# x updated earlier in one cross attention, a new order in grouped attention, and the last MX batch in pieces

## The reference

```python
x = x + _L0_attn_ref(_layernorm(x), Wqkv, Wout)                    # causal, 16 heads
x = x + _L0_xattn_ref(_layernorm(x), ctx, Wq, Wk, Wv, Wo, gq, gk)  # q and k normed by head
x = x + _L0_ffn_ref(_layernorm(x), router, shared, routed)
x = x + _L1_attn_ref(_layernorm(x), Wq, bq, Wk, bk, Wv, bv, Wo, bo) # 32 query heads in 8 groups
x = x + _L1_xattn_ref(_layernorm(x), ctx, mask, Wq, Wk, Wv, Wo)     # masked keys
x = x + _L1_ffn_ref(_layernorm(x), gate_w, up_w, down_w)            # MX
...
scales = jnp.maximum(max_abs / _FP8_MAX, _EPS)      # _mx_dequant, blocks of 32
q = (blocks / scales[..., None]).astype(jnp.float8_e4m3fn).astype(jnp.float32)
return (q * scales[..., None]).reshape(rows, feat)
```

## Time and profile before

| | |
|---|---|
| median of three runs | 1590.43 us |
| the profiled execution | 1583.99 us |
| its span on the core | 1582.2 us |
| PE busy | 1479.4 us, 93% |
| DVE busy | 1068.8 us, 68% |
| ACT busy | 968.4 us, 61% |
| POOL busy | 730.6 us, 46% |
| mean granted TensorE clock | 0.986 |

### The profile page before, as it was taken

One profiled execution on the slowest core, in us unless ns is written; L12 is line 12 of the kernel. 1 busy time (PEld: TensorE's weight loads), 2 busy tenths in 40 slices (PEclk: granted clock), 3 DMA queues, 4 the chain that ended last, 5 costly groups with the idle time before them and its releaser, 6 DMA issues. The chain is left out here.

```text
span 1582.2 us, 30300 instructions
## 1 busy us (share of the span) xinstructions
PE 1479.4 (93%) x10256; PEld 1214.4 (77%) x10256; DVE 1068.8 (68%) x2468; ACT 968.4 (61%) x2611; POOL 730.6 (46%) x893
## 2 busy tenths in 40 slices
PE   5999889999999999899987989899999999989998
PEld 2666568888888888688874555489999999977886
DVE  4667667878877787554446777655556665588886
ACT  2766657777777777433236777577777777642221
POOL 3666635555555555223333333213444434457775
PEclk9999999999999999999999999999999999999999
DMA  6000020000000000000011000020000000000000
GB/s 243 2 1 2 2 95 5 3 5 3 5 3 5 3 3 1 22 1 1 1 53 82 2 1 1 15 90 8 8 8 8 5 4 5 1 1 14 14 14 14
DMA packets 15609, 29.82 MB, mean 19 GB/s; under 512 B 1505, under 2 KB 12002, under 8 KB 14690
## 3 DMA queue, kind: packets, MB, share of 16 engines
q1 hardware_dynamic: 15458, 27.89, 4.8%
HBM read 25.79 MB, written 2.10 MB: 18 GB/s over the span
## 5 line engine op out<-in xcount | busy, mean ns | idle before, releaser
L1444 POOL TENSOR_TENSOR weights_even<-weights_even,cross_reciprocal 128x512 f32<-128x512 f32 x64 | 66.7, 1042 | 202.8 <-DVE cross_reciprocal L1676 202.8
L926 POOL TENSOR_TENSOR cross_work<-cross_work,cross_reciprocal 128x512 f32<-128x512 f32 x64 | 66.6, 1040 | 182.6 <-DVE cross_reciprocal L1083 182.6
L1526 ACT ACTIVATE weights_even<-bank,cross_shift 128x128 f32<-128x128 f32 x256 | 90.7, 366 | 80.0 <-DVE cross_shift L1668 80.0
L1149 PE MATMUL bank<-ident,cross_work 128*128 128x128 f32 x768 | 117.0, 275 | 2.4 <-DVE cross_work L1061 2.4
L979 ACT ACTIVATE cross_work<-bank,cross_shift,cross_q_rms 128x128 f32<-128x128 f32 x256 | 113.6, 456 | 2.2 <-DVE cross_shift L1055 2.2
L1149 PEld LDWEIGHTS bank<-ident,cross_work 128*128 128x128 f32 x768 | 90.5, 142 | 26.9 <-DVE cross_work L1061 18.0
L2468 DVE TENSOR_REDUCE grouped_maxima<-bank 128x4 bf16<-128x512 f32 x128 | 82.4, 685 | 34.5 <-PE bank L2550 26.9
L1953 POOL TENSOR_TENSOR mlp_low_inner<-mlp_inner,mlp_high_inner 128x512 fp32r<-128x512 f32 x36 | 48.7, 1354 | 117.1 <-ACT mlp_high_inner L1996 117.1
L1666 DVE TENSOR_REDUCE cross_maxima<-bank 128x4 f32<-128x512 f32 x64 | 44.2, 690 | 84.5 <-PE bank L1809 84.5
L402 POOL TENSOR_TENSOR causal_masked_maxima<-causal_maxima,causal_constants 128x512 bf16<-128x512 bf16 x64 | 67.0, 1068 | 55.7 <-DVE causal_maxima L547 55.7
L2808 ACT ACTIVATE mx_silu<-bank 128x512 f32<-128x512 f32 x32 | 19.1, 598 | 114.7 <-PE bank L2928 114.6
(11 more groups left out here) (365 smaller groups left out, 5332.9 us busy)
## 6 DMA issues: line engine op xcount, KB each, us to landing
weights_even<-in_weights SPq DMA_DIRECT2D x2, 2560.0 KB, 11.7
weights_even<-in_weights SPq DMA_DIRECT2D x2, 1732.0 KB, 8.6
weights_odd_early<-in_weights SPq DMA_DIRECT2D x1, 3072.0 KB, 11.7
weights_odd_values<-in_weights SPq DMA_DIRECT2D x1, 3072.0 KB, 18.5
weights_odd_late<-in_weights SPq DMA_DIRECT2D x2, 1536.0 KB, 10.0
x<-in_x SPq DMA_DIRECT2D x4, 512.0 KB, 8.1
...
```

The source lines that it names most:

```text
L926: pool.tensor_tensor(probs[x], probs[x], reciprocal[x][:, :].unsqueeze(2).to_broadcast([P, PER, P]), ALU.mult).then_inc(probs_divided, 1)
L1149: last = pe.transpose(bank[:, j * P:(j + 1) * P], source, core.ident[:, :])
L1444: pool.tensor_tensor(probs[x], probs[x], reciprocal[x][:, :].unsqueeze(2).to_broadcast([P, JOBS, P]), ALU.mult).then_inc(probs_divided, 1)
L1526: last = act.activation(probs[x][:, j, :], bank_scores[x][:, j * P:(j + 1) * P], ACT.Exp, scale=SCALE, bias=shift[x][:, j:j + 1], accum_ou ...
```

## The change

- In the first cross attention, DVE's update_x(t - 1) at g == 2 moves from after sum_q to ahead of row_maxima, right after make_low_heads.
- The scale step gets its two numbers from a new pair of columns in SBUF, scale_bounds, that POOL fills once in the setup. It is used in all places that scale.
- In grouped attention PE's order within a step becomes: key and query projections, scores (1, 1), weigh_values of the batch before (1), scores_transposed (0), turn_maxima (1), the values' projection, turn_out, project_heads, scores (0, 0) of the next batch, scores_transposed (1), scores (0, 1) of the next, turn_h, turn_heads, weigh_values (0), turn_maxima (0) of the next, scores (1, 0) of the next. The turned maxima of half 0 go to the bank bank_scoresT[0], which adds a wait for the exponential that last read it. DVE and ACT get a matching order: maxima (1, 1), statistics one batch later than before, spread (1), normalise_heads, update_x, the next batch's maxima (0, 0) and (0, 1), spread (0), maxima (1, 0); ACT's copy_outT goes ahead of the first four exponentials. POOL's rstd is one batch later.
- In the last batch of the MX MLP the second half is rounded by DVE in two pieces of 256 columns, instead of by POOL in one of 512; PE turns and ACT copies each piece by itself, and the down projection's matmuls go between. add_to_x of the batch before goes ahead of the rounding.

```diff
@@ -246,6 +247,8 @@
             pool.memset(core.ones_bf[:, :], 1.0)
+            pool.memset(core.scale_bounds[:, 0:1], 1.0 / FP8_MAX)
+            pool.memset(core.scale_bounds[:, 1:2], LEAST_SCALE)
             pool.memset(core.ones[:, :], 1.0).then_inc(made, 1)
@@ -755,11 +758,17 @@
-def dve_scale(dve, source, scratch, step, least, done):
+def dve_block_scale(dve, core, scratch):
+
+    return dve.tensor_scalar(scratch.scale[:, :], scratch.largest[:, :], core.scale_bounds[:, 0:1],
+                             core.scale_bounds[:, 1:2], ALU.mult, ALU.max)
+
+
+def dve_scale(dve, core, source, scratch, step, done):
...
                            ALU.max, apply_absolute_value=True))
-    step(dve.tensor_scalar(scratch.scale[:, :], scratch.largest[:, :], 1.0 / FP8_MAX, least, ALU.mult, ALU.max))
+    step(dve_block_scale(dve, core, scratch))
     step(dve.reciprocal(scratch.inverse[:, :], scratch.scale[:, :]))
@@ -1113,6 +1122,8 @@
                         make_low_heads(i - 2, g % 2)
+                    if g == 2 and batch_there(t - 1):
+                        update_x(t - 1)
                     if there(i):
@@ -1127,8 +1138,6 @@
                         sum_q(i + 1, (g + 1) % 2)
-                    if g == 2 and batch_there(t - 1):
-                        update_x(t - 1)
                     if there(i + 2):
@@ -2266,6 +2273,7 @@
         bank_scores, bank_scoresT, bank_out, bank_misc = core.banks[0:2], core.banks[2:6], core.banks[6], core.banks[7]
+        turned_maxima = [bank_scoresT[0][:, 0:P], bank_scores[0][:, 0:P]]
@@ -2424,11 +2432,11 @@
                     normalise(t + 2)
+                if batch_there(t - 1):
+                    copy_outT(t - 1)
                 if batch_there(t):
...
                         exponentials(t, 0, j)
-                if batch_there(t - 1):
-                    copy_outT(t - 1)
                 if batch_there(t + 1):
@@ -2475,7 +2483,7 @@
                     dve.tensor_tensor(shifts[c][:, :, :],
-                                      bank_scores[0][:, 0:P].unsqueeze(1).to_broadcast([P, PER, P]),
+                                      turned_maxima[c].unsqueeze(1).to_broadcast([P, PER, P]),
                                       row_of_member.unsqueeze(2).to_broadcast([P, PER, P]), ALU.mult)\
@@ -2510,20 +2518,20 @@
                 if batch_there(t):
-                    row_maxima(t, s, 1, 0)
                     row_maxima(t, s, 1, 1)
+                if batch_there(t - 3) and not left_to_next(t - 3):
+                    statistics(t - 3)
+                if batch_there(t):
                     spread_shifts(t, 1)
...
                     normalise_heads(t - 1)
-                if batch_there(t + 1):
-                    row_maxima(t + 1, 1 - s, 0, 0)
                 if batch_there(t - 2):
...
                 if batch_there(t + 1):
+                    row_maxima(t + 1, 1 - s, 0, 0)
                     row_maxima(t + 1, 1 - s, 0, 1)
                     spread_shifts(t + 1, 0)
-                if batch_there(t - 2) and not left_to_next(t - 2):
-                    statistics(t - 2)
+                    row_maxima(t + 1, 1 - s, 1, 0)
                 if isinstance(t, int) and t == -1:
@@ -2542,8 +2550,8 @@
                 pe.wait_ge(max_ready, nonneg(GROUPS * b + SLOTS * c + 2 * pair))
-                if pair == 0:
-                    pe.wait_ge(shifts_ready, nonneg(EC * b + c))
+                if c == 0 and pair == 0:
+                    pe.wait_ge(shifts_ready, nonneg(EC * b))
                 for j in range(2):
@@ -2562,7 +2570,9 @@
                 pe.wait_ge(max_ready, GROUPS * b + SLOTS * (c + 1))
-                pe.matmul(bank_scores[0][:, 0:P], maxima[s][:, c, :, :].rearrange("p j m -> p (j m)"),
+                if c == 0:
+                    pe.wait_ge(probs_ready, nonneg(GROUPS * b - SLOTS + 1))
+                pe.matmul(turned_maxima[c], maxima[s][:, c, :, :].rearrange("p j m -> p (j m)"),
                           core.minus_ident_bf[:, :], start=True, stop=True).then_inc(max_turned, 1)
@@ -2646,21 +2656,20 @@
                 if batch_there(t):
-                    scores(t, s, 1, 0)
-                    scores_transposed(t, s, 0)
                     scores(t, s, 1, 1)
...
                     weigh_values(t - 1, 1 - s, 1)
+                if batch_there(t):
+                    scores_transposed(t, s, 0)
+                    turn_maxima(t, s, 1)
                 if batch_there(t + 1):
...
                     project_values(t + 1)
-                if batch_there(t):
-                    turn_maxima(t, s, 1)
+                if batch_there(t - 1):
+                    turn_out(t - 1)
                 if batch_there(t - 2):
                     project_heads(t - 2)
-                if batch_there(t - 1):
-                    turn_out(t - 1)
                 if batch_there(t + 1):
@@ -2680,6 +2689,7 @@
                     turn_maxima(t + 1, 1 - s, 0)
+                    scores(t + 1, 1 - s, 1, 0)
             batches(pe, step)
@@ -2691,6 +2701,9 @@
     SCALE_STEPS = 5
+    VERY_LAST, PIECES = BATCHES - 1, 2
+    PIECE = INTER // HALVES // PIECES
+    TILES_A_PIECE = PIECE // P
     with ExitStack() as ctx:
@@ -2764,7 +2780,7 @@
                 pool.wait_ge(innerT_filled, nonneg(HALVES * (b - 1)))
-                for j in range(HALVES):
+                for j in range(HALVES if b != VERY_LAST else HALVES - 1):
                     pool.wait_ge(inner_scaled, HALVES * b + j + 1)
@@ -2819,6 +2835,13 @@
+            def copy_last_piece(k):
+                act.wait_ge(last_turned, k + 1)
+                first = TILES // HALVES + TILES_A_PIECE * k
+                act.activation(innerT[:, first:first + TILES_A_PIECE, :],
+                               last_banks[k][:, 0:PIECE].rearrange("p (i t) -> p i t", t=P),
+                               ACT.Copy).then_inc(last_copied, 1)
+
             fetch_h(0)
@@ -2827,8 +2850,11 @@
                         silu_of_gate(HALVES * (t - 1) + j, j)
-                    if batch_there(t - 2):
+                    if batch_there(t - 2) and (t - 2, j) != (VERY_LAST, 1):
                         copy_innerT(t - 2, j)
+                if t - 2 == VERY_LAST:
+                    for k in range(PIECES):
+                        copy_last_piece(k)
                 if isinstance(t, int) and t == 1:
@@ -2858,7 +2884,24 @@
                 dve.wait_ge(inner_rounded, nonneg(i - HALVES + 1))
-                dve_scale(dve, bank_gate[j][:, :], scratch[j], inner_step, LEAST_SCALE, inner_scaled)
+                dve_scale(dve, core, bank_gate[j][:, :], scratch[j], inner_step, inner_scaled)
+
+            def round_last_half():
+                dve.wait_ge(inner_scaled, HALVES * BATCHES)
+                dve.wait_ge(innerT_filled, HALVES * (VERY_LAST - 1))
+                for k in range(PIECES):
+                    part = slice(k * PIECE, (k + 1) * PIECE)
+                    blocks = slice(k * PIECE // BLOCK, (k + 1) * PIECE // BLOCK)
+                    scaled, rounder = scratch[1].scaled[:, part], scratch[1].rounder[:, part]
+                    dve.tensor_tensor(scaled, scaled, rounder, ALU.add).then_inc(last_chain, 1)
+                    dve.wait_ge(last_chain, 2 * k + 1)
+                    dve.tensor_tensor(scaled, scaled, rounder, ALU.subtract).then_inc(last_chain, 1)
+                    dve.wait_ge(last_chain, 2 * k + 2)
+                    dve.tensor_tensor(inner_q[VERY_LAST % 2][:, 512 + k * PIECE:512 + (k + 1) * PIECE]
+                                      .rearrange("p (b k) -> p b k", k=BLOCK),
+                                      scaled.rearrange("p (b k) -> p b k", k=BLOCK),
+                                      scratch[1].scale[:, blocks].unsqueeze(2)
+                                      .to_broadcast([P, PIECE // BLOCK, BLOCK]), ALU.mult).then_inc(last_rounded, 1)
@@ -2884,7 +2927,7 @@
                                              core.rstd[:, LEFT_BY_PAIR:], ALU.mult, ALU.mult).then_inc(shift_ready, 1)
-                if batch_there(t - 3):
+                if batch_there(t - 3) and t - 3 != VERY_LAST - 1:
                     add_to_x(t - 3, 1 - s)
@@ -2896,6 +2939,9 @@
                         scale_inner(i, j)
+                    if t - 1 == VERY_LAST:
+                        add_to_x(t - 2, s)
+                        round_last_half()
                 elif batch_there(t):
@@ -2953,7 +2999,41 @@
+            def down_tiles(tiles):
+                for m in tiles:
+                    last = pe.matmul(bank_y[:, 0:EMBED], innerT[:, m, :], w_down[:, m, :],
+                                     start=(m == 0), stop=(m == TILES - 1))
+                return last
+
+            def last_batch(s):
+
+                half = TILES // HALVES
+
+                def tiles_of(k):
+                    return range(half + TILES_A_PIECE * k, half + TILES_A_PIECE * (k + 1))
+
+                def turn_piece(k):
+                    pe.wait_ge(last_rounded, k + 1)
```

(19 more changed lines are left out.)

16 lines of the change are left out of this document (9 added, 7 removed).

## The result

The changed kernel takes 1571.99 us in the median of 5 runs (1566.97 to 1572.84), the kernel before 1589.61 in the median of its 5 (1584.12 to 1590.57). The ratio is 0.990, with an interval of 0.9879 to 0.9921: 15.9 us less, between 12.6 and 19.2. The forecast was 18.8 less. Time and mean granted clock went together: of 27 further executions of the kernel before, eight took 1590 to 1591 us at 0.979 to 0.982 and the others 1582 to 1587 at 0.983 to 0.988, and of the changed kernel's five, three took 1572 to 1573 at 0.984 and two 1567 to 1568 at 0.990 and 0.991. The span of the changed kernel in the profiled execution is 1570.6, with a mean granted clock of 0.984.

The account below looks back on a forecast made before the run. PE was taken as full in the first cross attention and steady MX stage, a chain across engines as bounding grouped attention. 4.0 + 4.8 + 3.0 + 2.0 + 0.5 + 4.5 = 18.8 off 1590.4 gave 1571.6, range 1560 to 1584.

Parts of the forecast that it names:

- Part 1: First cross attention: update_x earlier, PE gains about 0.27 a batch, 15 times, 4.0 us less (nothing to 10.7).
- Part 2: Grouped attention: new order cuts a batch from 11.29 to 10.85 us; 4.8 us less (nothing to 9).
- The walk: Grouped attention: new order timed step by step from the key and query projections, next start at 10.85 us.
- the three chains that end together: Grouped attention: narrowed keys, maxima of s10 and mx01 arrive just in time, so nothing beyond 0.44 without all.
- Rival D: Grouped attention: the order closes a slow ring through ACT; 24 us slower there, 1600 in all; chance 0.03.
- Part 3: Scale step with SBUF scalars takes 0.18 to 0.2 us: masked cross 3.0, MX start 2.0, steady MX 0.5.
- rival A: Scale step still waits for POOL; takes 5.5 away, 13.3 us less in all, 1577; chance 0.13.
- L143's row: Profile row taken, against the Trainium skill's rule, as evidence that SBUF scalars spare the scale step POOL's wait.
- Part 4: Last MX batch: DVE's pieces replace POOL's passes and PE's 3.44 us wait; 4.5 us less.
- warm end: Last MX batch: down projection's matmuls at 0.216 us each, end at 1576.7, 5.5 us less.
- Rival B: DVE becomes the bound in first cross and grouped attention; 10.0 us less gained, 1580; chance 0.17.
- C: Better: update_x's whole 0.71 returns (10.7) and grouped attention runs at 10.6 (8.3); 1561; chance 0.08.

Follow-up runs that it names:

- cross1_alone: The kernel before with only update_x moved in the first cross attention; ratio 0.9959 (0.9943 to 0.9975), 6.5 us less.
- stats_split: The changed kernel with the first cross attention's statistics split, first pass at g == 2, rest at g == 3; 13 distances 340.10 us instead of 342.88.
- grouped_alone: The kernel before with only the new order in grouped attention; ratio 0.9952 (0.9935 to 0.9969), 7.6 us less.
- update_between: The changed kernel with grouped attention's update_x back between DVE's maxima (0, 0) and (0, 1); 10.61 us a batch, 12 distances 127.36 instead of 132.98.
- port_times: The kernel before plus DVE operations timed alone and beside POOL; numbers or columns take 710 and 709 ns beside its multiply, numbers 294 beside its power.

## Why the prediction was right, and where not

The total fits (1571.99 against 1571.6), and the parts do not: two were too small, one too large, and one gave nothing. That it fits to 0.4 us is luck. Terms that were too small made good most of a part that gave nothing, and 1571.6 was counted from 1590.43, the median of three executions, where 27 further ones gave 1584.97; by the ratio the gain is 15.9, and 18.8 was forecast.

**Part 1**, forecast 4.0: 8.3 from the first add_output to the last, of which 14 x 0.5 = 7.1 in the steady distances and 1.2 at the last batch's wait (7.16, now 5.92); cross1_alone 6.5 (4.0 to 9.0). The mechanism held. The wait of L1239 for x is gone, and PE waits for DVE one group later, at the turn of k: 1.84 after the turn ahead of it in the group of update_x (393.76 to 395.60), 2.02 after it in the next one (400.18 to 402.20). The term that was too small is "PE gains 0.36 less 0.1, about 0.27 a batch"; it measured 0.49. The 0.1 was no cost: from make_low_heads to the maxima it is 0.96 with update_x between them (393.00 to 393.96) and without (390.74 to 391.70). And the 0.36 is idle time from DVE's recorded end, while on DVE the maxima can start 0.61 after the start of make_low_heads, ahead of its end (400.05 to 400.66), so that the room from start to start was 0.45. Two records of the kernel before show what was not in the sum:

```profile
396.16 0.69 DVE L1048 TENSOR_REDUCE cross_k_sums<-cross_work 128x4 f32<-128x512 f32 x1
...
397.80 0.69 DVE L1072 TENSOR_TENSOR cross_low_heads<-bank,cross_high_heads 128x512 fp32r<-128x512 f32 x1
```

397.80 + 0.61 is 398.41, 0.45 ahead of the 398.86 of the earlier trace rows. The old place of update_x gave DVE nothing: sum_k starts 1.07 after sum_q with update_x between them (395.09 to 396.16), and 1.06 after it without (397.35 to 398.41), since it then waits for ACT. stats_split brings the other 0.22 of the 0.72.

**Part 2**, forecast 4.8: in the trace 2.4 in the steady part, less 1.0 at the end, and 1.8 at the joint, 3.2 in all; grouped_alone 7.6 (4.9 to 10.3), the difference explained only in part by the other pieces of its trace. The 1.8 at the joint was nowhere in the forecast; in its own stage the part gave 1.4. The walk itself held: counted from the projections at 903.20 (914.28 less a period), update_x starts at 7.03 (walk 6.95), the maxima at 7.36 (7.3), the second scores at 8.70 (8.65), the turn of the maxima at 10.60 (10.58). The term that was too small is the last: turn and s10 take 0.48 up to the next projections, not 0.27, so 11.08 and not 10.85. That update_x would wait for the values' copy was right by 0.05: POOL's bias comes later by that. The walk had the bias nowhere, though it names POOL's narrowing ahead of it. The end gave back 1.0 where I had a gain of 0.5. And where I wrote that nothing beyond 0.44 is to be had, update_between got 0.68 by one exchange on DVE: the three chains that end together did so only in the order I had walked. Rival D's slow ring did not come about: after its copy of outT ACT still waits 0.46 for the transposed scores (at 918.99), and the handover from DVE's maxima to PE takes 0.06 (ended at 911.84, PE at 911.90), as forecast.

**Part 3**, forecast 5.5: nothing, and rival A came true, to which I gave 0.13. The step that failed is the reading of L143's row "never long though POOL works beside it". What stood beside it in 15 of the 16 cases was POOL's power of 128 x 4 (L921), which holds nothing up, as port_times shows, and its 405 against 295 ns is the price of two columns (0.12), not another kind of access. I took a longer duration for another mode. The masked stage's 3.0 fell with it (its steady time changed by 0.19), and the MX stage lost 0.8 where 2.5 was to be gained.

**Part 4**, forecast 4.5: 5.4 in the traces with the clock at 1.00, 3.8 where it fell, 4.6 (2.1 to 7.1) measured. The warm end of that term (5.5) was seen in seven traces of nine. The cold one (2.7) was not: in the other two the clock fell for a part of the stretch only.

So the sum, 8.3 + 3.2 - 0.8 + 5.4 = 16.1 by the traces (0.8 is what the MX stage loses), agrees with the measured 15.9 (12.6 to 19.2), and the forecast's 18.8 is still inside: the parts were off by +4.3, -1.6, -6.3 and +0.9, which leaves only 2.7 in the sum. The spans of the two traces differ by less, 11.6, because the changed kernel's execution lost 3.1 and 1.7 at two joints where its clock was lower. Rival B did not come true in either stage, and C in part for part 1 (8.3 of its 10.7); its period of 10.6 in grouped attention came only with update_between.
